# Three token tiles by gathered rows, and masks kept with the row of a group outermost, in a sparse feed-forward layer

## The chip, the cores and the metric

The kernel runs on one core of one Trainium2 chip. The metric is the device time of one launch in microseconds (us), the median of three runs. One more execution was taken with the hardware profiler; its rows are shown below, and all times inside the kernel come from it.

## What is computed

`x` is 16 x 100 x 1024, 1600 tokens. A cross-attention layer is added to it first; this text is about the sparse feed-forward layer behind it:

```python
def ffn(x, c1_w, c2_w, w1, w2t):              # 1600 tokens, DIM 1024, INTER 3584, SPARSITY 64, RANK 16
    inter = xf @ c1_w.T @ c2_w.T              # gate values, 1600 x 3584
    blk = inter.reshape(B * T, n_blocks, 64)  # 56 groups of 64 rows for each token
    idx = argmax(blk, axis=-1) + arange(0, INTER, 64)
    w1_g, w2_g = w1[idx], w2t[idx]            # one row of 64 is taken, for each token and group
    h = relu(einsum('bkm,bm->bk', w1_g, xf))
    return einsum('bk,bkm->bm', h, w2_g)
x = x + xattn(layernorm(x), ctx)
x = x + ffn(layernorm(x), c1_w, c2_w, w1, w2t)
```

## The kernel before

The layer is computed in two ways side by side. The tokens stand in tiles of 128; the first `S` tiles are the "sparse tiles", the rest go the dense way.

**The dense way.** `hidden_layer` multiplies the dense tokens with all 3584 rows of `w1` and closes what the gate did not choose; `project_down` multiplies the result with all of `w2t`. `w1` comes in 28 blocks of 128 rows, two of which are a pair (one pass of `body`, 14 in all). Each block is turned by TensorE (`turn_w`, L1669), and split into a high part by ScalarE (`high_part`, L1752) and a low part by VectorE (`low_part`, L1786). `sums` (L1698) is 24 matmuls (8 chunks x 3 products of high and low parts) over one of four column tiles of 336 tokens; `close` (L1689) adds a large negative number where the mask is set, as small bf16 matmuls with the mask as the stationary operand; ScalarE takes the tile out with Relu (`evacuate`, L1761), and it is stored in `h_scratch`.

**The masks.** For each pair TensorE makes the gate values of all 13 token tiles in four portions (`gates`, L1680; 4, 4, 4 and 1 tiles) in one two-bank tile of PSUM, so a portion waits until the one before has been read (the semaphore `compared`). On VectorE `pick` takes the maximum of each 64 (L1800), compares (L1802, writes bf16), multiplies by a falling key (L1804), takes the largest key (L1808), and `mark` compares again (L1817). All of the portion's four groups of a tile lie behind each other with the 64 rows innermost. `body` makes the masks of pair i + 1 while TensorE works on pair i, and `close` of the first tile of a pair waits for all its masks (`masked`).

**The gathered way.** For the S = 2 sparse tiles `SparseTiles` gathers, for each tile and each of 56 groups, the chosen row of `w1` for each token by an indirect DMA of GpSimd (L1529, 128 rows of 4 KB), and VectorE multiplies it with the token and sums (`dot`, L1536); later the chosen row of `w2t` is gathered and added with that weight (`axpy`, L1544). That is 112 dots and 112 sums. 78 dots (6 for each of 13 pairs) are done in `hidden_layer`, through a ring of 4 rows; 34 dots and all sums are spread over the units of `project_down`, through a ring of 6 rows. A row's buffer is gathered again when the step that read it is done.

**The second product.** `project_down` (L2376) goes in three passes over 28 chunks, with 11 token tiles in each (10 of 128 and one of 64), 66 units in all. ScalarE makes the high parts (L2292, L2283), VectorE the low parts (L2315, L2308), up to four units ahead of TensorE. The sparse steps stand between them in VectorE's order.

Each engine runs its instructions in the order in which they are written.

## Time and profile before

| what | us |
|---|---|
| median of three runs | 3539.28 (3535.36 to 3540.3) |
| profiled execution, its own time | 3539.46 |
| its span, first to last instruction | 3537.8 |
| hidden layer, about | 2605 to 3108 |
| second product, about | 3108 to 3538 |

A row of grouped instructions gives line, engine, operation, output and inputs with their shapes, how many, then busy time in us, the mean length of one in ns, and the idle time ahead of them with what ended it. Instructions of one engine overlap at their ends: the distance from start to start is what one costs when the engine is full, and is read from the timeline. "PE" is TensorE's matmuls, "PEld" its weight loads, "DVE" VectorE, "ACT" ScalarE, "POOL" GpSimd, "SPq" and "POOLq" transfers issued by SyncE and GpSimd.

### The profile page before, as it was taken

How to read it: one execution, taken by the hardware profiler on the slowest of the kernel's cores; microseconds unless marked ns; L12 is line 12 of the kernel's file. 1: busy time of each engine (PE TensorE's matmuls, PEld its weight loads, DVE VectorE, ACT ScalarE, POOL GpSimd, SP SyncE). 2: the span in 40 equal slices, each digit the busy share in tenths (PEclk: the TensorE clock that was granted, in tenths of full speed). 3: DMA queues.
4: the chain of work that ended last, by engine and by line, in shares of the span. 5: the costliest groups of instructions: out<-in, count | busy, mean ns of one | idle time of the engine just before them, and what ended most of it. 6: DMA issues, size and time to landing. Idle time of an engine off the chain costs nothing. (4 is left out here: it accounts for less than half of the span.)

```text
span 3537.8 us, 51963 instructions
## 1 busy us (share of the span) xinstructions
PE 3419.9 (97%) x18422; PEld 3044.1 (86%) x18422; DVE 2248.0 (64%) x3746; ACT 1372.0 (39%) x2610; POOL 877.6 (25%) x1108
## 2 busy tenths in 40 slices
PE   6999999799999999999999899999989999999999
PEld 5888888699999899999999778788789999977877
DVE  5555567677866577777777523433277787766775
ACT  4333344344433577777777422322231111121120
POOL 0000000000000477777776100000011111144543
PEclk8999999899999999999999999999999999999999
DMA  3333332354444334444333654544334444589786
GB/s 119 106 97 104 96 108 84 96 141 125 118 117 124 109 106 112 111 113 113 107 94 87 193 126 121 178 130 120 106 125 149 153 166 156 172 314 310 259 292 215
DMA packets 477970, 501.72 MB, mean 142 GB/s; under 512 B 172580, under 2 KB 372260, under 8 KB 477764
## 3 DMA queue, kind: packets, MB, share of 16 engines
q1 hardware_dynamic: 441988, 371.79, 36.0%
q0 software_dynamic: 34720, 125.19, 10.2%
q8 instruction: 117, 1.92, 0.2%
q10 hardware_dynamic: 1056, 2.10, 0.2%
q14 instruction: 89, 0.73, 0.1%
HBM read 383.98 MB, written 115.02 MB: 141 GB/s over the span
## 5 line engine op out<-in xcount | busy, mean ns | idle before, releaser
L2087 PE MATMUL wo_acc<-wo_w,wo_l 128*128 128x512 f32 (+1 forms) x2496 | 577.4, 393 | 17.0 <-DVE wo_l L2037 16.9
L269 PE MATMUL kv_bank<-kv_wo,kv_so 128*128 128x512 f32 x2436 | 575.0, 395 | 15.4 <-DVE kv_wo L361 11.1
L2087 PEld LDWEIGHTS wo_acc<-wo_w,wo_l 128*128 128x128 f32 (+1 forms) x2496 | 462.1, 186 | 132.2 <-DVE wo_w L2061 16.9
L269 PEld LDWEIGHTS kv_bank<-kv_wo,kv_so 128*128 128x128 f32 x2436 | 457.9, 190 | 110.4 <-issue 16.7
L657 PE MATMUL pr_bank<-pr_xo,pr_wp 128*128 128x400 f32 x2688 | 498.7, 347 | 29.0 <-ACT pr_s L724 13.4
L657 PEld LDWEIGHTS pr_bank<-pr_xo,pr_wp 128*128 128x128 f32 x2688 | 493.5, 190 | 31.8 <-DVE pr_wp L741 24.0
L1698 PE MATMUL hid_acc<-x1t,hid_w 128*128 128x336 f32 x2688 | 440.0, 319 | 0.0
L2376 PE MATMUL w_acc<-w_w,w_l 128*128 128x512 f32 (+1 forms) x1848 | 421.3, 390 | 5.2 <-DVE w_l L2315 5.2
L1698 PEld LDWEIGHTS hid_acc<-x1t,hid_w 128*128 128x128 f32 x2688 | 415.7, 189 | 1.1
L2376 PEld LDWEIGHTS w_acc<-w_w,w_l 128*128 128x128 f32 (+1 forms) x1848 | 339.0, 184 | 87.1 <-DVE w_l L2315 5.3
L2037 DVE TENSOR_TENSOR wo_l<-wo_l_raw,wo_l 128x512 fp32r<-128x512 f32 (+1 forms) x208 | 139.3, 671 | 344.5 <-ACT wo_l L2010 344.3
L27 PE MATMUL scores<-kt,q_parts 128*128 128x462 f32 x1152 | 338.7, 402 | 1.7 <-ACT probs L1218 1.7
L1089 POOL TENSOR_SCALAR probs<-probs,inverse 128x461 f32<-128x461 f32 x400 | 261.9, 655 | 210.0 <-DVE inverse L1256 172.4
L2010 ACT ACTIVATE wo_l<-wo_l_raw 128x512 fp32r<-128x512 f32 (+1 forms) x208 | 127.5, 614 | 408.5 <-PE wo_acc L2087 379.9
L1218 ACT ACTIVATE probs<-scores,negmax 128x461 f32<-128x461 f32 x400 | 258.0, 645 | 37.6 <-DVE negmax L1249 36.5
L1249 DVE TENSOR_REDUCE negmax<-scores 128x1 f32<-128x461 f32 x400 | 250.9, 627 | 23.8 <-PE scores L1126 23.2
L1142 PE MATMUL turned<-ident,probs 128*128 128x128 f32 x1600 | 241.1, 273 | 1.2 <-POOL probs L1089 1.2
L1142 PEld LDWEIGHTS turned<-ident,probs 128*128 128x128 f32 x1600 | 203.1, 142 | 20.2 <-POOL probs L1089 1.6
L1761 ACT ACTIVATE c_raw<-hid_acc 128x336 f32<-128x336 f32 x112 | 50.2, 452 | 392.1 <-PE hid_acc L1689 392.1
L27 PEld LDWEIGHTS scores<-kt,q_parts 128*128 128x128 f32 x1152 | 190.1, 192 | 10.7 <-ACT probs L1218 2.0
L1260 DVE TENSOR_TENSOR pt_first<-turned,pt_first 128x512 fp32r<-128x512 f32 x192 | 132.1, 688 | 86.2 <-ACT pt_first L1212 85.0
L1529 POOL DMA_INDIRECT w_ring<-in_L_ffn_w2t_dram,idx x112 | 141.8, 1266 | 162.8 <-DVE w_ys L1544 55.1
(194 smaller groups left out, 4581.0 us busy)
## 6 DMA issues: line engine op xcount, KB each, us to landing
wo_l_raw<-o_scratch SPq DMA_DIRECT2D x192, 256.0 KB, 2.9
pair_raw<-in_L_xattn_Wq_dram SPq DMA_DIRECT2D x64, 512.0 KB, 6.0
q_scratch<-pr_out SPq DMA_DIRECT2D x128, 200.0 KB, 2.6
o_scratch<-o_stage SPq DMA_DIRECT2D x64, 400.0 KB, 3.7
q_raw<-q_scratch SPq DMA_DIRECT2D x64, 384.0 KB, 3.1
stage<-in_ctx_dram SPq DMA_DIRECT2D x45, 512.0 KB, 4.0
h_scratch<-c_raw SPq DMA_DIRECT2D x28, 672.0 KB, 3.2
wo_w_raw<-in_L_xattn_Wo_dram SPq DMA_DIRECT2D x16, 1024.0 KB, 7.0
```

What stands on the lines that cost most here:

```text
L27: last = pe.matmul(out, left(a, c), right(b, c), start=(c == 0 and (a, b) == PAIRS[0]), stop=(c == chunks - 1 and (a, b) == PAIRS[-1]))
L269: last = pe.matmul(bank[:, BANK[i], :], so[:, i, a, c, :], wo[:, i, e, c, :], start=(not opened and c == 0 and (a, e) == PAIRS[0]), stop=( ...
L657: last = pe.matmul(bank[:, BANK[i], :width], wo[:, i, a, c, :], xo[:, i, e, c, :], start=(not opened and c == 0 and (a, e) == PAIRS[0]), s ...
L1089: pool.tensor_scalar(probs[:, I % RB, :kv], probs[:, I % RB, :kv], inverse[:, I % RB:I % RB + 1], 1.0, ALU.mult, ALU.mult).then_inc(scaled, 1)
L1142: last = pe.transpose(turned[:n, j % TB, k, :], probs[:, j % RB, at:at + n], ident[:, :])
L1218: act.activation(probs[:, I % RB, :kv], scores[:, I % SB, :kv], ACT.Exp, bias=negmax[:, I % RB:I % RB + 1], accum_out=total[:, I % RB:I % ...
L1249: dve.tensor_reduce(negmax[:, I % RB:I % RB + 1], scores[:, I % SB, :kv], AX.X, ALU.max, negate=True).then_inc(s_max, 1)
L1529: return pool.indirect_dma_start(row[:, :], None, (self.w1 if kind == "in" else self.w2t)[:, :], bass.IndirectOffsetOnAxis(self.idx[:, s, ...
L1698: pe.matmul(acc[:, t, :width], w[p][:, a, c, :], x1t[:, b, c, skip + t * width:skip + (t + 1) * width], start=(c == 0 and (a, b) == PAIRS[ ...
L2037: dve.tensor_tensor(l[j % 2][:, 1, :, :rows], l_raw[j % 2][:, :, :rows], l[j % 2][:, 0, :, :rows].bitcast(F32), ALU.subtract).then_inc(l_l ...
L2087: last = pe.matmul(acc[p][:rows, :], l[j % 2][:, a, k, :rows], w[:, c, m * per + k, :], start=(m == 0 and k == 0 and (a, c) == PAIRS[0]), ...
L2376: last = pe.matmul(acc[:heights[t], n % AB, h * cols:(h + 1) * cols], l[u % LB][:, a, k, :heights[t]], w[:, b, c % slots_w, h * cols:(h + ...
```

## The change

- S is 3: three token tiles go by gathered rows. The dense tokens are 1216 in place of 1344: a column tile has 304 columns in place of 336, and the second product has 10 token tiles in place of 11 (9 of 128 and one of 64), 60 units. Dots and sums are 168 each.
- All 168 dots are in `hidden_layer`, with one sum in each of 12 pairs: 180 steps for 13 pairs, 12 to 14 in one. The other 156 sums are in `project_down`. Both rings have 5 rows. The sums' accumulators (`totals`) are loaded at the start of `hidden_layer`.
- The masks are laid out with the row of a group outermost and the tiles' groups innermost, in two halves of 8 and 5 tiles. After the maximum (`largest`) ScalarE compares: one `Sign` activation for each tile and group (16 for a portion, 4 for the last) with the negated maximum as bias. VectorE then works on a half at a time: `keyed` adds the key, `halved` and `quartered` take maxima of the halves, `leading` reduces the 16 values left, `mark` compares. The leading key is bf16 now.
- ScalarE's `Sign` groups stand between its `evacuate` and `high_part`.
- The order of VectorE's work in a pair is written anew, with the steps between the parts of the masks.
- The normalised third tile is kept, and x1t holds the dense tokens alone.

```diff
-    R_HIDDEN, R_DOWN, PER_PAIR = 4, 6, 6
+    R_HIDDEN, R_DOWN, SUMS = 5, 5, 1
...
+            def signs(i, k):
+                a, n = picks[k]
+                x_half, at = divmod(2 * a, spans[0])
+                act.wait_ge(topped, NP * i + k + 1)
...
+                for x in range(n * per):
+                    last = act.activation(equal[x_half][:, x % pair, :, at + x // pair], values[:, x, :], ACT.Sign,
+                                          bias=top[:, a * per + x:a * per + x + 1])
+                last.then_inc(compared, 1)
...
+                    evacuate(i, p, 0)
...
+                    if another:
+                        high_part(j + 1, 1 - p, 0)
+                    if more and not late:
+                        signs(i + 1, 2 * p)
+                    evacuate(i, p, 1)
...
+                    if another:
+                        high_part(j + 1, 1 - p, 1)
+                    evacuate(i, p, 2)
+                    if more:
+                        signs(i + 1, 2 * p + 1)
+                    evacuate(i, p, 3)
...
-                dve.tensor_tensor(equal[:, at, :], values, spread(top[:, at], g), ALU.is_equal).then_inc(compared, 1)
...
+            def keyed(i, x):
+                dve.wait_ge(compared, NP * i + 2 * x + 3)
+                dve.tensor_tensor(equal[x][:, :, :, :], equal[x][:, :, :, :], key_bf[:, :, :spans[x]].rearrange(
+                    "q (b c) a -> q b c a", b=1).to_broadcast([P, pair, sparsity, spans[x]]), ALU.add).then_inc(step, 1)
+            def halved(i, x):
+                n, g = sparsity // 2, spans[x]
+                dve.wait_ge(step, 4 * (2 * i + x) + 1)
+                dve.tensor_tensor(half[:, :, :, :g], equal[x][:, :, :n, :], equal[x][:, :, n:, :], ALU.max).then_inc(step, 1)
...
+            def tree(i, m, x, between):
+                keyed(i, x)
+                steps(between[:1])
+                halved(i, x)
+                quartered(i, x)
+                steps(between[1:2])
+                leading(i, x)
+                steps(between[2:3])
+                mark(i, m, x)
+                if x == 0:
+                    indices(i)
...
+            def body(i, m, more):
+                mine = list(sparse.body[i])
+                cuts = (0, 2, 4, 9, 10, 10, len(mine)) if more else (0, 3, 6, 9, 12, 15, len(mine))
+                a, b, c, d, e, f = [mine[cuts[n]:cuts[n + 1]] for n in range(6)]
+                if i > 1:
+                    dve.wait_ge(clipped, i - 1)
+                low_part(2 * i + 1, 1, 0)
+                if more:
+                    largest(i + 1, 0)
+                steps(a)
+                low_part(2 * i + 1, 1, 1)
+                steps(b)
+                if more:
+                    largest(i + 1, 1)
+                steps(c)
+                if more:
+                    low_part(2 * i + 2, 0, 0)
+                    largest(i + 1, 2)
+                    tree(i + 1, 1 - m, 0, d)
+                    low_part(2 * i + 2, 0, 1)
+                    steps(e)
+                    largest(i + 1, 3)
+                    tree(i + 1, 1 - m, 1, f)
+                    steps(f[3:])
+                else:
+                    steps(d + e + f)
+                clip(i)
...
-        S = 2
+        S = 3
```

## Rows read from the trace of the kernel before

**Rows 1.** The page's first part: busy time, share of span, instructions of each engine.

```profile
PE 3419.9 (97%) x18422; PEld 3044.1 (86%) x18422; DVE 2248.0 (64%) x3746; ACT 1372.0 (39%) x2610; POOL 877.6 (25%) x1108
```

**Rows 2.** Windows: length, busy time of the engines, clock, DMA share, GB/s.

```profile
2605.00:3108.00 503.00, 494.95 (x3486) 477.30 (x3486) 388.08 (x523) 85.61 (x172) 78.83 (x81) 0.99 0.44 151
3130.00:3200.00 70.00, 70.00 (x310) 58.01 (x309) 55.50 (x64) 8.40 (x12) 50.28 (x37) 1.00 1.01 373
3200.00:3300.00 100.00, 100.00 (x442) 79.42 (x441) 72.07 (x83) 20.02 (x25) 43.19 (x35) 1.00 0.85 280
```

**Rows 3.** TensorE's timeline in the hidden layer: start, length, group, idle before.

```profile
2608.16 1.19 PE L1680 MATMUL gate<-c2s,zs 112*128 112x256 f32 x4 [1.77 <-DVE hid_w L1786]
...
2653.54 0.63 PE L1669 MATMUL turn<-ident,w_raw 128*128 128x128 f32 x4
...
2895.29 3.95 PE L1698 MATMUL hid_acc<-x1t,hid_w 128*128 128x336 f32 x24
2899.08 0.32 PE L1689 MATMUL hid_acc<-closed,hid_mask 128*128 128x128 bf16 x3
2899.24 0.63 PE L1669 MATMUL turn<-ident,w_raw 128*128 128x128 f32 x4
2899.62 0.72 PE L1680 MATMUL gate<-c2s,zs 112*128 x4
...
2930.39 0.88 PE L1698 MATMUL hid_acc<-x1t,hid_w 128*128 128x336 f32 x4
...
3108.82 9.54 PE L2376 MATMUL w_acc<-w_w,w_l 128*128 128x512 f32 x34 [5.18 <-DVE w_l L2315]
```

**Rows 4.** Groups of the second product, 3108 to 3538.

```profile
L2376 PE MATMUL w_acc<-w_w,w_l 128*128 128x512 f32 x1680 | 383.0, 390 | 5.2 <-DVE w_l L2315 5.2
L1544 DVE SCALAR_TENSOR_TENSOR w_ys<-w_ring,value,w_ys 128x1024 f32<-128x1024 f32 x112 | 140.1, 1280 | 12.4 <-DMA w_ring<-in_L_ffn_w2t_dram,idx 12.3
```

**Rows 5.** VectorE's timeline in one pair.

```profile
2894.55 1.22 DVE L1536 CUSTOM_DVE_ANT_0 c_raw<-c_raw,keep 128x1024 f32<-128x1024 f32 x1
...
2895.70 1.22 DVE L1536 CUSTOM_DVE_ANT_0 hid_ring<-hid_ring,keep 128x1024 f32<-128x1024 f32 x1
...
2900.53 0.69 DVE L1786 TENSOR_TENSOR hid_w<-turn,hid_w 128x512 fp32r<-128x512 f32 x1 [3.40 <-ACT hid_w L1752]
2901.14 1.21 DVE L1800 TENSOR_REDUCE hid_top<-gate 128x16 f32<-128x1024 f32 x1
```

**Rows 6.** VectorE's groups in the hidden layer, shapes apart.

```profile
L1808 DVE TENSOR_REDUCE hid_lead<-hid_equal 128x16 f32<-128x1024 bf16 x42 | 51.2, 1220 | 1.4
L1817 DVE TENSOR_TENSOR hid_mask<-hid_equal,hid_lead 128x1024 bf16<-128x1024 bf16 x42 | 51.2, 1218 | 0.6
L1800 DVE TENSOR_REDUCE hid_top<-gate 128x16 f32<-128x1024 f32 x42 | 51.1, 1218 | 8.8 <-PE gate L1680 8.8
L1804 DVE TENSOR_TENSOR hid_equal<-hid_equal,hid_key_bf 128x1024 bf16<-128x1024 bf16 x42 | 29.1, 692 | 1.4
L1808 DVE TENSOR_REDUCE hid_lead<-hid_equal 128x4 f32<-128x256 bf16 x14 | 5.9, 420 | 0.5
L1804 DVE TENSOR_TENSOR hid_equal<-hid_equal,hid_key_bf 128x256 bf16<-128x256 bf16 x14 | 4.1, 292 | 0.5
```

**Rows 7.** ScalarE's groups: two of the hidden layer, two of the attention.

```profile
L1761 ACT ACTIVATE c_raw<-hid_acc 128x336 f32<-128x336 f32 x112 | 50.2, 452 | 392.1 <-PE hid_acc L1689 392.1
L1752 ACT ACTIVATE hid_w<-turn 128x512 fp32r<-128x512 f32 x56 | 33.3, 598 | 25.0 <-PE turn L1669 24.0
...
L1218 ACT ACTIVATE probs<-scores,negmax 128x461 f32<-128x461 f32 x400 | 258.0, 645 | 37.6 <-DVE negmax L1249 36.5
...
L1190 ACT ACTIVATE kt<-kb 128x461 fp32r<-128x461 f32 x60 | 33.4, 557 | 0.0
```

**Rows 8.** ScalarE's timeline in the attention, two neighbours.

```profile
1501.72 0.59 ACT L1212 ACTIVATE pt_first<-turned 128x512 fp32r<-128x512 f32 x1
1502.20 0.65 ACT L1218 ACTIVATE probs<-scores,negmax 128x461 f32<-128x461 f32 x1
```

**Rows 9.** Transfers of the hidden layer: queues (packets, MB, share of 16 engines), issue to landing.

```profile
q0 software_dynamic: 11232, 40.90, 23.4%
q1 hardware_dynamic: 9465, 34.97, 20.7%
...
rows_raw<-in_L_ffn_w_dram,idx POOLq DMA_INDIRECT x38, 5.9
```

**Rows 10.** Transfers of the second product.

```profile
q0 software_dynamic: 21024, 76.56, 50.2%
q1 hardware_dynamic: 46439, 44.99, 32.2%
...
w_ring<-in_L_ffn_w_dram,idx POOLq DMA_INDIRECT x34, 7.0
```

**Rows 11.** TensorE's weight loads in the hidden layer.

```profile
L1698 PEld LDWEIGHTS hid_acc<-x1t,hid_w 128*128 128x128 f32 x2688 | 415.7, 189 | 1.1
...
L1689 PEld LDWEIGHTS hid_acc<-closed,hid_mask 128*128 128x128 bf16 x392 | 21.2, 98 | 16.1 <-DVE hid_mask L1817 0.5
```

**Rows 12.** The one table load of ScalarE after 2450.

```profile
L1433 ACT ACT_TABLE_LOAD x1 | 1.3, 1283 | 9.8 <-PEq L1902 9.8
```

More of the change, by code:

```diff
@@ L1315, in sb @@
             return mem.enter_context(nc.sbuf_tensor("mid_" + n, shape, dt))
[L1317 removed]
+        ring = list(lent) + [sb(f"raw{i}", [P, hidden]) for i in range(R - len(lent))]
         raw = [keep[t] if t < len(keep) else ring[t % R] for t in range(NT)]
@@ L1517, in __init__, with earlier @@
         sums = [("out", n % S, n // S) for n in range(S * groups)]
-        count = self.PER_PAIR * (groups // per - 1)
-        self.hidden, late = dots[:count], dots[count:]
-        self.down = []
-        for n, step in enumerate(sums):
-            self.down += late[len(late) * n // len(sums):len(late) * (n + 1) // len(sums)]
-            self.down.append(step)
-        self.pairs = groups // per - 1
-        where = {step: k for k, step in enumerate(self.down)}
-        assert all(("in", s, g) not in where or where["in", s, g] < where["out", s, g] for _, s, g in sums)
+        bodies = groups // per - 1
+        self.hidden, self.body = [], [range(0)]
+        for b in range(bodies):
+            first = len(self.hidden)
+            mine = dots[len(dots) * b // bodies:len(dots) * (b + 1) // bodies]
+            assert mine[-1][2] // per <= b + 1
+            self.hidden += mine
+            if b:
+                self.hidden += sums[self.SUMS * (b - 1):self.SUMS * b]
+            self.body.append(range(first, len(self.hidden)))
+        self.down = sums[self.SUMS * (bodies - 1):]
+    def earlier(self, steps, k):
+        return max([j for j in range(k) if steps[j][:2] == steps[k][:2]], default=None)
     def gather(self, pool, kind, s, g, row):
@@ L1565, in hidden_layer @@
     NP = len(picks)
+    assert NP == 4
+    pair = per // 2
+    spans = [sum(n for _, n in picks[2 * x:2 * x + 2]) * 2 for x in range(2)]
+    most = max(spans)
     parts = [[] for _ in range(tiles)]
@@ new lines, in steps, with first_pair @@
+            def steps(some):
+                for k in some:
+                    sparse_step(k)
+            def tree(i, m, x, between):
[9 more added lines that the diff above has]
+                    indices(i)
+            def first_pair():
+                for x in range(2):
+                    largest(0, 2 * x)
+                    largest(0, 2 * x + 1)
+                    tree(0, 0, x, ())
+                low_part(1, 1, 0)
+                low_part(1, 1, 1)
+                largest(1, 0)
+                largest(1, 1)
+                low_part(2, 0, 0)
+                largest(1, 2)
+                low_part(2, 0, 1)
+                tree(1, 1, 0, ())
+                largest(1, 3)
+                tree(1, 1, 1, ())
```

241 lines of the change are left out of this document (112 added, 129 removed).

## The prediction

> **What bounds the kernel now.** I read the page first: TensorE is busy for 97% of the span [rows 1]. The windows say the same of the two stages that the change touches: 495 of 503 us in the hidden layer, and 70 of 70 us in a stretch of the second product where the DMA engines are full [rows 2]. The timeline then gives the hidden layer's period. Pairs start at 2895.29 and 2930.39, 35.10 us apart, and nothing on TensorE waits between them [rows 3]. So before the change a column that TensorE does not compute is worth its time, as long as the other engines can follow. The question is whether they can, because the change gives them more.
>
> **What TensorE gets back.** In the second product 1848 matmuls of 512 columns are 168 for each of 11 token tiles; 383.0 us for 1680 is 0.228 us each [rows 4]. One tile fewer saves 168 x 0.228 = 38.3 us. In the hidden layer a tile of 24 matmuls of 336 columns takes 3.79 us to its close [rows 3], 0.158 us each. Between 336 and 512 columns a matmul grows by (228 - 158) / 176 = 0.40 ns a column; a column per cycle of the granted 2.4 GHz would be 0.42. For 32 columns I take 0.0133 us: 0.32 us for each of 112 tiles, 2.56 us a pair, 35.8 us in all. The closes are 26 for a pair, not 28, 0.1 us. TensorE's own pair would be 32.4 us.
>
> **What VectorE is given in a pair.** Costs from start to start. A dot is 1.15 us (2894.55 to 2895.70), a low part 0.61 (2900.53 to 2901.14) [rows 5]. From the lengths, less 0.08 of overlap: three maxima at 1.13 and one at 0.35, 3.75. The bf16 operations: the multiply takes 692 ns for 1024 elements and 292 for 256, which is 0.52 ns an element on 160 ns; the others (a reduce, or an f32 operand) take 1220 and 420, 1.04 ns an element on 160 [rows 6]. `keyed` and `mark` work on 2048 and 1280 bf16 elements: 1.15 and 0.75 each at the fast rate; 2.2 and 1.4 at the slow one. I take the fast one, because all operands are bf16 with the innermost step of one, as in the multiply. `halved` and `quartered` 0.73, 0.46 and 0.52, 0.25; `leading`, a reduce at the slow rate, 0.72 and 0.41. Indices 0.3, clip 0.2. The 13.85 steps (180 / 13) at 1.15 are 15.9. With 2.4 for low parts the sum is 29.5 us, before any wait. That is under 32.4, but VectorE's order is fixed, so the waits must be laid out.
>
> **What ScalarE is given.** A `Sign` of 64 columns reads PSUM with a bias for each partition. The activation of 461 columns with such a bias takes 645 ns, without it 557, and a column is 0.83 ns (598 against 452 for 512 and 336) [rows 7]: 0.65 - 397 x 0.00083 = 0.32 us. Two neighbours overlap by 0.11 (0.59 long, 0.48 apart) [rows 8], so 0.22 us apart. It could be 0.32 if the strided bf16 output stops the overlap, hardly less than 0.19. 52 in a pair are 11.4 us; with evacuations and high parts ScalarE has about 17 us. It is not the bound, but 16 in a row hold up what stands behind them for 3.5 us.
>
> **The pair, laid out.** Time 0 is the first low part of a body. `largest` 0 ends at 1.8; its 16 signs to 5.4, the evacuation 5.7, the high part 6.3: the second low part, which VectorE reaches at 4.0, starts at 6.4. A wait of 2.3. Two steps to 9.3, `largest` 1 to 10.4, then five steps. Here the ring of 5 counts: the fourth needs the buffer of a step that ended at 8.2. An indirect DMA takes 5.9 us to land at today's load and 7.0 in the second product [rows 9, 10]; the load will be near the latter, so I take 7.1 with the issue. The row is there at 15.3, a wait of 1.4. Five steps end at 17.6. Low part, `largest` 2, the first tree with its step, indices, low part: 25.6. `largest` 3 with its four signs holds `keyed` for 1.1 until 27.1. The second tree, with three steps, has its mask at 33.3. Now the close of the next pair's first tile runs, then `turn_w`, and the low part 1.29 us after that has begun (2899.24 to 2900.53) [rows 3, 5]: 0.05 + 0.16 + 1.29 on 33.3 is 34.8. TensorE reaches this close 3.47 us into its pair and waits some 2 us for it. So the pair is 34.8 us, set by maxima, signs, rows and masks, not by TensorE's 32.4. Of the 2.7 us saved, 0.3 is left. Bounds: 33.4 if rows never wait; 36.8 if signs are 0.32 apart (1.6 more) and rows land a little later.
>
> **Start and end of the hidden layer.** Before, 45.4 us lie between the first gate portion and the turn ahead of the first steady pair [rows 3]. Then no step is there to fill in. Each portion must wait for the one before to be reduced and compared, 1.2 + 3.5 us against 4.1 of TensorE's work, and the third portion's maximum is written behind the first tree, so TensorE idles some 5.5 us there; the masks come 6 us later than before. In the second pass three portions wait 1.5 us each and the first tree starts behind `high_part`, behind 16 signs; the close waits 3 us more. Less the shorter tiles this is 11 us lost (7 to 15). The last pair has no masks: 7 tiles after its first close save 2.2 us. Its 14 steps, at 5 rows in 8.3 us, end before TensorE does, so the next stage starts as before, 5.2 us after [rows 3].
>
> Hidden layer: +11 - 12 x 0.3 - 2.2 = +5 us.
>
> **The second product.** 156 sums in some 390 us. A gather holds the 16 DMA engines for 50.2% x 430 / 146 = 1.48 us; 156 of them are 231 us, and the rest, 32.2% x 430 less the eleventh tile, 128: 0.91 of the stage where it was 0.82 [rows 10]. In the first pass a step is due every 2.2 us, where 37 came in 70 us, 1.9 each, with TensorE full [rows 2]. VectorE's sum is 1.20, as long as 1.28 less the overlap [rows 4]. So this stage stays TensorE's, and I give 1 us to the first units, where rows come late. -37.
>
> Sum: 3539.5 + 5 - 37 = 3507.5, say 3508; the profiled execution and the median are the same within 0.2 us.
>
> **Two rules of the Trainium skill.** The masks are now read and written with a step of 32 or 20 bytes. No row shows that; a mask's load is 98 ns, an f32 block's 189 [rows 11], so at worst of these 26 closes cost 2.4 us more a pair, TensorE's 32.4 becomes 34.8, and the sum does not move but for 2 us of the last pair. The Trainium skill, "SBUF — State Buffer" (Door 1: The DMA port swizzle, its note on cachelines), says that each access that crosses to a new line pays a penalty, without a price; by it the closes, the signs and `leading` would all be slower than I count, and the sum larger by what that costs. Second, ScalarE's tables: after 2450 one load stands in the trace, 1283 ns ahead of the square root, and Copy and Relu alternate without any [rows 12]. The Trainium skill, "ScalarE: Activation LUTs" (Table sets: the hidden batching unit), says that a function of another set needs a load, and names Relu, Copy and Abs as in every set, but not Sign.
>
> **Rivals.**
> - A. As forecast: the small operations hold the pair at 34 to 36 us, the second product pays. 3498 to 3523. 57%.
> - B. The waits are shorter than I lay out (rows at 4 to 5 us, signs at 0.19), and TensorE bounds the pair at 32.4 to 33.2: 12 x 2.3 us less than 34.8, so 3480. For it: in the hidden layer the engines have room today [rows 2]. Against: the five steps in a row. 15%.
> - C. Slower than before: the bf16 operations on the new layout run at the slow rate. `keyed`, `halved`, `quartered`, `mark` cost 1.07 + 0.53 + 0.27 + 1.07 for the larger half and 0.67 + 0.33 + 0.16 + 0.67 for the smaller, 4.8 us, all in the chain: 39.6 us a pair, 12 x 4.8 + 4 at the start, 3569. It decides from a pair of 37.5 us on (37 - 11 + 2.2 = 28 us over 12 pairs). 10%.
> - D. Transfers: rows land 10 us after release; a pair is 37, and in the second product TensorE waits 8 us: 3508 + 26 + 8 = 3542. For it: 0.80 of the DMA engines in the hidden layer (13.85 x 1.51 + 7 in 34.8 us) against 0.44, with fewer rows in flight. 13%.
> - E. Sign stands in another table than Relu and Copy, and each change between them costs the 1283 ns of the row [rows 12]: two changes in each of the two sign groups on the path, 5.1 us a pair: 3508 + 61 = 3569. The trace shows nothing of Sign; for that Relu and Copy could be had beside it, one load would do and this falls away. 5%. It is the case that the rule of the Trainium skill's "ScalarE: Activation LUTs" leaves open.
>
> **Chances.** What this kernel's measurement can tell is about 0.2%, 7 us. Faster: A, B and a little of D, 0.80. Same 0.06, slower 0.14. The range takes in most of B and part of D: 3484 to 3536; the likeliest case alone is 3498 to 3523.
>
> **What would show it.** Right: pairs start 34 to 36 us apart, with one wait of about 2 us on the mask at the first close; VectorE over 90% busy in the hidden layer; `Sign` 0.22 apart; `mark` 1.2 us for 2048 elements; the second product 38 us shorter with TensorE full. Wrong: `mark` at 2.3 us (C), VectorE waiting for rows by several us a pair (D), table loads (E), pairs at 32.5 us (B), or a hidden layer whose start is not about 11 us longer.

## The result and the profile after

The changed kernel takes 3547.87 us (median of 11 runs, 3544.39 to 3551.22); the kernel before, measured beside it, 3539.52 (11 runs). The ratio is 1.0025, 95% interval 1.0015 to 1.0034: slower by some 8 us, just more than the 0.2% that can be told from no change. The forecast was 3508. The profiled execution took 3546.57 us with a span of 3544.9, 7.1 us more than before.

I read the stages first. The page's first part, beside [rows 1]:

```profile
PE 3365.6 (95%) x18226; PEld 2996.3 (85%) x18226; DVE 2272.8 (64%) x3815; ACT 1576.9 (44%) x3332; POOL 1065.9 (30%) x1220
```

TensorE has 54 us less to do and the span has not become shorter, so it waits. The windows, with the columns of [rows 2]: 505 us of the hidden layer, 59 us near its start, and the first 155 us of the second product.

```profile
2605.00:3110.00 505.00, 454.43 (x3254) 438.14 (x3255) 386.40 (x619) 286.08 (x887) 228.56 (x171) 0.96 0.68 236
2613.00:2672.00 59.00, 44.87 (x266) 43.24 (x266) 22.75 (x33) 34.72 (x116) 4.92 (x5) 0.82 0.19 66
3145.00:3300.00 155.00, 150.38 (x642) 120.45 (x643) 113.92 (x103) 29.80 (x37) 82.41 (x62) 0.96 0.96 335
```

In the hidden layer 50 us are idle on TensorE where 8 were [rows 2], and in the 59 us near its start the granted clock is 0.82. Laid against the trace of before, by the points that the forecast used (us; "turn" is the turn that follows a pair's first close):

| stretch | before | after | difference | forecast |
|---|---|---|---|---|
| first gate portion starts at | 2608.16 | 2610.98 | +2.8 | (in the next) |
| from there to the turn of the first steady pair | 45.38 | 65.12 | +19.7 | +11 |
| 12 pairs, turn to turn, mean of one | 35.10 | 36.40 | +15.7 | -3.6 |
| last pair, from its turn to its last close | 28.46 | 26.32 | -2.1 | -2.2 |
| from there to the second product | 5.63 | 6.28 | +0.7 | 0 |
| second product, first to last matmul | 420.88 | 390.01 | -30.9 | -37 |
| behind it | 8.06 | 9.30 | +1.2 | 0 |

The sum is +7.1, all of the difference between the spans. For the runs below, "start" and "pairs" are taken one tile of sums earlier, at the tile that stands ahead of a pair's first close: the start is 41.42 before and 59.20 here, and the pairs are 35.10 and 36.40 again.

Now one pair, on VectorE's timeline (start, length, line, operation, idle ahead). Its time 0 is 2931.11. Left out are mostly dots of 1.15 us each.

```profile
2931.11 0.69 DVE L1848 TENSOR_TENSOR hid_w<-turn,hid_w 128x512 fp32r<-128x512 f32 x1 [0.37 <-ACT hid_w L1779]
2931.71 1.21 DVE L1857 TENSOR_REDUCE hid_top<-gate 128x16 f32<-128x1024 f32 x1
...
2938.46 0.69 DVE L1848 TENSOR_TENSOR hid_w<-turn,hid_w 128x512 fp32r<-128x512 f32 x1 [3.25 <-ACT hid_w L1779]
...
2948.20 1.23 DVE L1546 CUSTOM_DVE_ANT_0 rows_raw<-rows_raw,keep 128x1024 f32<-128x1024 f32 x1 [1.05 <-DMA rows_raw<-in_L_ffn_w_dram,idx]
...
2949.36 0.69 DVE L1848 TENSOR_TENSOR hid_w<-turn,hid_w 128x512 fp32r<-128x512 f32 x1
...
2957.74 0.41 DVE L1857 TENSOR_REDUCE hid_top<-gate 128x4 f32<-128x256 f32 x1
2959.65 0.83 DVE L1862 TENSOR_TENSOR hid_equal<-hid_equal,hid_key_bf 128x1280 bf16<-128x1280 bf16 x1 [1.49 <-ACT hid_equal L1800]
...
2965.25 0.82 DVE L1883 TENSOR_TENSOR hid_mask<-hid_equal,hid_lead 128x1280 bf16<-128x1280 bf16 x1
...
2967.71 0.69 DVE L1848 TENSOR_TENSOR hid_w<-turn,hid_w 128x512 fp32r<-128x512 f32 x1 [0.36 <-ACT hid_w L1779]
```

It is the pair that was laid out, each wait at its place: low part 0, behind the signs at 7.35 (forecast 6.4); a row waited for, 1.05 (1.4); the third low part at 18.25 (17.6); the fourth maximum at 26.6 (25.6); `keyed` held 1.49 (1.1); the mask done at 34.96 (33.3); the next body at 36.60 (34.8). TensorE's timeline shows the wait at the end, ahead of the first close, and on ScalarE's stands what makes the first one:

```profile
2966.13 0.37 PE L1716 MATMUL hid_acc<-closed,hid_mask 128*128 128x128 bf16 x3 [2.25 <-DVE hid_mask L1883]
```

```profile
2932.96 4.74 ACT L1800 ACTIVATE hid_equal<-gate,hid_top 128x64 bf16<-128x64 f32 x16 [1.96 <-issue]
2937.20 0.76 ACT L1788 ACTIVATE c_raw<-hid_acc 128x304 f32<-128x304 f32 x1
```

Sixteen signs keep ScalarE for 4.24 us, 0.265 apart and not 0.22. The evacuation behind them takes 0.63 us up to the high part, where the forecast had 0.3.

TensorE's own work in such a pair, its length less its idle time, is 33.1 to 33.3 us. In five of the 12 pairs a part of it runs at 1.2 GHz behind the wait at the first close, and it is 34.4 to 34.6 us.

The groups, shapes apart (2610 to 3142), give the prices of the masks:

```profile
L1800 ACT ACTIVATE hid_equal<-gate,hid_top 128x64 bf16<-128x64 f32 x728 | 223.1, 761 | 124.7 <-DVE hid_top L1857 115.6 <-issue 9.1
...
L1883 DVE TENSOR_TENSOR hid_mask<-hid_equal,hid_lead 128x2048 bf16<-128x2048 bf16 x14 | 17.2, 1225 | 0.5
L1862 DVE TENSOR_TENSOR hid_equal<-hid_equal,hid_key_bf 128x2048 bf16<-128x2048 bf16 x14 | 17.0, 1217 | 4.7 <-ACT hid_equal L1800 4.7
L1877 DVE TENSOR_REDUCE hid_lead<-hid_quarter 128x32 bf16<-128x512 bf16 x14 | 16.7, 1189 | 0.5
```

`mark` and `keyed` run at the fast rate as forecast. `leading`, 512 elements, takes 1.19 where 0.69 would follow from the length. The start of the layer, on TensorE (the second to fourth tile of sums and what stands ahead of each):

```profile
2618.26 0.71 PE L1707 MATMUL gate<-c2s,zs 112*128 112x256 f32 x4 [1.89 <-ACT hid_equal L1800]
2618.81 3.50 PE L1725 MATMUL hid_acc<-x1t,hid_w 128*128 128x304 f32 x24
2625.00 1.19 PE L1707 MATMUL gate<-c2s,zs 112*128 112x256 f32 x4 [2.69 <-ACT hid_equal L1800]
2625.99 5.79 PE L1725 MATMUL hid_acc<-x1t,hid_w 128*128 128x304 f32 x24
2635.99 0.55 PE L1707 MATMUL gate<-c2s,zs 112*128 112x256 f32 x1 [4.22 <-ACT hid_equal L1800]
2636.35 5.73 PE L1725 MATMUL hid_acc<-x1t,hid_w 128*128 128x304 f32 x24
```

After idles of 2.69 and 4.22 us 24 matmuls take 5.8 us in place of 3.5: the granted clock has gone from 2.4 to 1.2 GHz. Up to the first steady pair six idles on ScalarE's signs add to 14.1 us (1.89, 2.69, 4.22, 2.19, 0.69, 2.39), and five slow tiles (4.39, 5.79, 5.73, 5.12, 5.03, each less 3.5) to 8.6. The first of these tiles stands behind an idle of 3.76 us ahead of the first portion. The second product, on TensorE:

```profile
3145.56 138.51 PE L2469 MATMUL w_acc<-w_w,w_l 128*128 128x512 f32 x600 [5.78 <-DVE w_l L2418]
3288.13 12.20 PE L2469 MATMUL w_acc<-w_w,w_l 128*128 128x512 f32 x42 [4.06 <-DVE w_w L2411]
```

The first pass is 10 of the 28 chunks, 600 matmuls for 10 token tiles. So the one wait, 4.06 us, stands between the first pass and the second, ahead of the new weights (`w_w`). Behind it 42 matmuls take 12.2 us where 42 x 0.228 is 9.6; the granted clock there is 1.2 GHz again. What led to the wait, on ScalarE and VectorE:

```profile
3281.66 0.74 ACT L2395 ACTIVATE w_l<-rows_raw 128x640 fp32r<-128x640 f32 x1 [4.24 <-DMA rows_raw<-h_scratch]
3282.31 1.04 ACT L2386 ACTIVATE w_w<-w_raw 128x1024 fp32r<-128x1024 f32 x1
...
3283.18 1.28 DVE L1554 SCALAR_TENSOR_TENSOR total<-w_ring,value,total 128x1024 f32<-128x1024 f32 x1
...
3284.37 2.47 DVE L1554 SCALAR_TENSOR_TENSOR total<-keep,value,total 128x1024 f32<-128x1024 f32 x2
...
3286.76 1.22 DVE L2411 TENSOR_TENSOR w_w<-w_raw,w_w 128x1024 fp32r<-128x1024 f32 x1
```

The weights themselves were there. Late was a tile of `h`, 12.3 us from its issue (3269.38) to its use, which holds ScalarE. Then the high part of the weights is ready at 3283.35, and VectorE starts their low part at 3286.76, because three sums stand ahead of it in its order.

### The profile page after: what moved, and what is told of

Its sections match the earlier page's. It is cut to its first block and busy times, and to the rows that moved or that the text cites. A ratio compares the mean times of both kernels' runs of the same rounds, so it can differ in the third digit from the quotient of the medians.

```text
span 3544.9 us, 52710 instructions
## 1 busy us (share of the span) xinstructions
PE 3365.6 (95%) x18226; PEld 2996.3 (85%) x18226; DVE 2272.8 (64%) x3815; ACT 1576.9 (44%) x3332; POOL 1065.9 (30%) x1220
## 5 line engine op out<-in xcount | busy, mean ns | idle before, releaser
L1725 PE MATMUL hid_acc<-x1t,hid_w 128*128 128x304 f32 x2688 | 411.7, 310 | 0.1
L2469 PE MATMUL w_acc<-w_w,w_l 128*128 128x512 f32 (+1 forms) x1680 | 386.3, 393 | 9.8 <-DVE w_l L2418 5.8
L1725 PEld LDWEIGHTS hid_acc<-x1t,hid_w 128*128 128x128 f32 x2688 | 391.2, 195 | 1.3 <-DVE hid_w L1848 0.3
L2469 PEld LDWEIGHTS w_acc<-w_w,w_l 128*128 128x128 f32 (+1 forms) x1680 | 309.4, 184 | 86.4 <-DVE w_l L2418 5.9
L1800 ACT ACTIVATE hid_equal<-gate,hid_top 128x64 bf16<-128x64 f32 x728 | 223.1, 761 | 124.7 <-DVE hid_top L1857 115.6
L1218 ACT ACTIVATE probs<-scores,negmax 128x461 f32<-128x461 f32 x400 | 258.2, 646 | 38.0 <-DVE negmax L1249 36.8
L2100 POOL DMA_DIRECT2D x_scratch<-wo_y x26 | 14.5, 557 | 577.3 <-DVE wo_y L2154 555.5
```

What stands on the lines that cost most here:

```text
L1218: act.activation(probs[:, I % RB, :kv], scores[:, I % SB, :kv], ACT.Exp, bias=negmax[:, I % RB:I % RB + 1], accum_out=total[:, I % RB:I % ...
L1725: pe.matmul(acc[:, t, :width], w[p][:, a, c, :], x1t[:, b, c, t * width:(t + 1) * width], start=(c == 0 and (a, b) == PAIRS[0]), stop=False)
L1800: last = act.activation(equal[x_half][:, x % pair, :, at + x // pair], values[:, x, :], ACT.Sign, bias=top[:, a * per + x:a * per + x + 1])
L2469: last = pe.matmul(acc[:heights[t], n % AB, h * cols:(h + 1) * cols], l[u % LB][:, a, k, :heights[t]], w[:, b, c % slots_w, h * cols:(h + ...
```

## The experiments

All are the changed kernel with one edit, unless it says otherwise; times are medians, ratios are against the kernel before.

My theory: the forecast's mechanisms are the right ones and its prices too low. The chain of signs, maxima, rows and masks in VectorE's order holds each pair (36.4 against TensorE's 33.3), and the start adds idle time that costs the clock as well. Rivals: TensorE's work itself has become longer by the stepped mask loads; the transfers hold the pair; the prices of the small operations alone do it, in any order.

**e1: small operations by themselves.** A kernel that computes nothing of the reference: groups of 16 activations of 64 columns, 16 reduces, and 64 loads and matmuls.

> A kernel of its own that measures single operations and computes nothing of the layer (its output is zeros). ScalarE, 16 at a time, 64 columns from PSUM: Sign with a bias for each partition to bf16 with a step of 16; the same to bf16 in a row; Relu without such a bias in a row, and with a step; Copy in a row; Sign from SBUF. VectorE: 16 reduces of 512 bf16 elements to 32 with the 16 that are reduced a step of 16 apart, then with them in a row. TensorE: 64 bf16 matmuls of 128 columns whose stationary operand is in a row, has a step of 16, or of 10. In the changed kernel 16 Sign are 4.24 us from the first to what follows, 0.265 apart, and the reduce of 512 took 1.20 us. If the stepped write is what costs, the first group is 0.26 apart and the second 0.22; if the function or the bias costs, both are 0.26 and Relu 0.19 or less. The reduce: 1.2 with the step, 0.69 in a row if the step costs; 1.2 both if bf16 output or shape does. Mask loads: in the changed kernel a close of three takes 0.05 us longer; expected 0.06 apart in a row and 0.075 with a step.

ScalarE's timeline: L112 is Sign with a bias into places 32 bytes apart, L116 the same in a row, L120 Relu without bias in a row, L124 that with the step.

```profile
6.85 4.53 ACT L112 ACTIVATE wide<-values,bias 128x64 bf16<-128x64 f32 x16
11.41 3.38 ACT L116 ACTIVATE flat<-values,bias 128x64 bf16<-128x64 f32 x16
14.82 1.97 ACT L120 ACTIVATE flat<-values 128x64 bf16<-128x64 f32 x16
16.82 4.44 ACT L124 ACTIVATE wide<-values 128x64 bf16<-128x64 f32 x16
```

```profile
L100 DVE TENSOR_REDUCE lead<-wide 128x32 bf16<-128x512 bf16 x16 | 15.7, 1056 | 22.4 <-ACT wide L132 22.4
...
L103 DVE TENSOR_REDUCE lead<-flat 128x32 bf16<-128x512 bf16 x16 | 9.6, 675 | 0.0
```

A sign is 0.255 us apart from the next with the stepped output, 0.20 in a row; Relu 0.25 and 0.10. With the step the bias makes no difference, so it is the stepped write that sets the pace. A reduce of 512 values costs 0.97 us stepped and 0.59 in a row. The mask loads with their matmuls were 62 ns apart with the step of 16 and 59 with that of 10 (medians). Of the block in a row the first 38 were 107 ns apart, and the rest 56: between them the granted clock rose from 1.2 to 2.4 GHz.

**e2: another order in the pair.** Each half's masks are finished before steps stand behind them, and the two halves' signs have five steps for cover.

```diff
-                steps(a)
+                steps(mine[:5])
                 low_part(2 * i + 1, 1, 1)
-                steps(b)
...
-                steps(c)
+                steps(mine[5:10])
...
-                    tree(i + 1, 1 - m, 0, d)
+                    tree(i + 1, 1 - m, 0, ())
                     low_part(2 * i + 2, 0, 1)
-                    steps(e)
                     largest(i + 1, 3)
-                    tree(i + 1, 1 - m, 1, f)
-                    steps(f[3:])
+                    steps(mine[10:11])
+                    tree(i + 1, 1 - m, 1, ())
+                    steps(mine[11:])
```

> The changed kernel with VectorE's order in a pair alone altered: five steps ahead of the second low part, five behind the second maximum, none inside the trees, one between the last maximum and its keyed, the rest behind the last mask. Same work, same rows, same rings. Theory 1 (the pair's length is the chain maximum, signs, trees with steps between, mask, close, turn, low part): the mask is there before TensorE asks for it, the pair falls from 36.4 to 33 us, TensorE waits under 0.5 us a pair, 3507. Rival 2 (rows and transfers set the pace): the same 14 rows come through the same ring, pairs stay over 35.5 us, 3537 to 3548. Rival 3 (TensorE is slower by the stepped mask loads and idles for other reasons): pairs 36, no change.

3522.57 us, ratio 0.9963 (0.995 to 0.9977). Pairs are 34.35 us, 2.05 less, with every operation and every transfer as before the edit; start (59.3) and second product (392.9) hardly moved. The theory had 33 us and 3507, so little more than half of its gain came. The list of waits of 2680 to 3100 says what changed. In the changed kernel (engine, what for, us, times, longest):

```profile
DVE hid_w L1848 <- ACT hid_w L1779: 44.7, 24, 3.3
...
PE hid_acc L1716 <- DVE hid_mask L1883: 22.8, 11, 2.2
```

In e2 the wait on the mask is gone and the second has shrunk; rows are waited for instead, 9.1 + 5.6 + 4.8 us:

```profile
DVE hid_w L1848 <- ACT hid_w L1779: 9.2, 12, 0.8
DVE rows_raw L1546 <- DMA rows_raw<-in_L_ffn_w_dram,idx: 9.1, 14, 2.5
```

So it is not the prices alone, nor TensorE's work: the order around them made them wait for each other. In these 12 pairs TensorE is never at the low clock, where five of the changed kernel's are in part.

**e3: another order at the start.** Three maxima go ahead of the first tree, the third portion's signs of pair 1 stand behind the high part, and VectorE takes up the wait for GpSimd's keys behind its first low parts.

```diff
-                for x in range(2):
-                    largest(0, 2 * x)
-                    largest(0, 2 * x + 1)
-                    tree(0, 0, x, ())
+                for k in range(3):
+                    largest(0, k)
+                dve.wait_ge(made, 2)
+                dve.wait_ge(base_made, 1)
+                tree(0, 0, 0, ())
+                largest(0, 3)
+                tree(0, 0, 1, ())
```

> The changed kernel with the start of the hidden layer alone altered: the third maximum of the first pair ahead of the first tree, the wait for the keys that GpSimd makes ahead of the first tree and not ahead of the first low part, and ScalarE's high part ahead of the third group of signs in the second block. Theory: gate values to the first steady turn falls from 65.1 to about 55 us (4.6 for the tree, 3 for the keys, the rest clock): 3536. Rival (16 signs in a row and the half clock bound the start whatever the order): 3545 or more.

3538.06 us, ratio 1.0002 (0.9993 to 1.0011). The start is 55.5, 3.7 less, and pairs stay at 36.2. From the first portion to the first steady turn are 59.1 us, where the theory had 55. The first portion starts at 2607.2, 3.7 us sooner, but only 1.3 of this is the edit's: from the layer's first turn to the first portion are 3.52 us here, 4.83 in the changed kernel and 2.83 before. The rest is an earlier start of the whole layer in this execution.

**e4: the masks alone.** S is 2 as before; masks, signs and order are as in the changed kernel, and all dots (112 now) are in the hidden layer.

```diff
-        S = 3
+        S = 2
```

> The changed kernel with S = 2 (two sparse tiles, 112 dots and 112 sums, all dots in the first product; one more row buffer of its own, as the borrowed one is too short): the masks, ScalarE's compares and the order without the third tile. Theory 1: nothing waits on masks in a steady pair, pairs 35.1 + 0.6 for the stepped mask loads = 35.7; the start is 22 us longer than before; the second product is 421 us as before: 3540 + 22 + 7 = 3569. Then the third tile is worth 21 us and the masks cost 29. Rival (the third tile itself costs more than it gives): 3547 or less.

3573.35 us, ratio 1.0101 (1.0086 to 1.0117): 36 us slower than before. The third tile by itself then gives some 27 (an estimate, from the two ratios). The second product is 421.3, as before; the start is 58.6, as in the changed kernel, so that all of its loss belongs to the masks. The pairs are 35.85, all alike but for the first, and on TensorE nothing waits in them:

```profile
2944.69 0.39 PE L1716 MATMUL hid_acc<-closed,hid_mask 128*128 128x128 bf16 x3
2944.91 0.64 PE L1696 MATMUL turn<-ident,w_raw 128*128 128x128 f32 x4
...
2963.60 3.85 PE L1725 MATMUL hid_acc<-x1t,hid_w 128*128 128x336 f32 x24
```

Three closes now take 0.22 us up to the next operation, where they took 0.16 [rows 3], and the whole pair 35.85 where it was 35.10 with the same tiles: the stepped masks cost TensorE 0.75 us a pair. The rival of the longer TensorE work has that much of it; in the changed kernel it makes 32.4 into some 33.1, still under the chain. e5 below bears it out with masks in a row: there three closes take 0.15 us, and TensorE's own work in a pair at full clock is 32.2 us.

**e5: the row of a group innermost.** The signs write in a row, `leading` reads in a row, and the masks lie as before the change; the maxima by halves and the order stay.

```diff
-        equal = [sb(f"equal{x}", [P, pair, sparsity, g], BF16) for x, g in enumerate(spans)]
+        equal = [sb(f"equal{x}", [P, g * pair, sparsity], BF16) for x, g in enumerate(spans)]
...
-                    last = act.activation(equal[x_half][:, x % pair, :, at + x // pair], values[:, x, :], ACT.Sign,
+                    last = act.activation(equal[x_half][:, 2 * at + x, :], values[:, x, :], ACT.Sign,
```

> The changed kernel with the masks laid out as before it, the 64 rows innermost, and all else kept (maximum by halves, ScalarE's Sign, bf16 key and lead). Signs are then written in a row: 16 in 3.4 us, not 4.3 (the single operations were 0.20 and 0.25 apart); the reduce 0.4 and 0.25 us shorter; mark spreads its lead over the innermost axis and goes at the slow rate, 1.07 and 0.67 us longer. Theory (these single prices add up along the chain): a steady pair 36.4 - 0.85 - 0.15 - 0.65 + 1.75 = 36.5, the start 5 us shorter for its signs and 2.6 for the keys: 3540. If only mark matters the pair is 38 and it is 3567; if only the signs matter 35.5 and 3530.

3537.84 us, ratio 1.0004 (0.9995 to 1.0013). The start is 50.2, 9 us shorter; the pairs are 36.37, as long as in the changed kernel, and the second product is 391.5. The groups show a bargain with a loss: sixteen signs take 3.38 us, `leading` 0.69, but `mark` has doubled.

```profile
L1799 ACT ACTIVATE hid_equal<-gate,hid_top 128x64 bf16<-128x64 f32 x728 | 154.9, 358 | 120.9 <-DVE hid_top L1856 113.9 <-issue 7.1
...
L1882 DVE TENSOR_TENSOR hid_mask<-hid_equal,hid_lead 128x2048 bf16<-128x2048 bf16 x14 | 32.1, 2291 | 0.5
...
L1876 DVE TENSOR_REDUCE hid_lead<-hid_quarter 128x32 bf16<-128x512 bf16 x14 | 9.6, 686 | 0.5
```

Here `mark`'s second operand repeats one value along the innermost axis, 2.29 us for 2048; in the changed kernel it is repeated along a middle one, 1.22. The Trainium skill, "VectorE: DVE Perf Modes" (Mode 2×_1P), wants 16-bit operands with a step of one for the double rate; both rows agree.

**e6: 52 sums left out.** Of the second product's sums those of the third tile are not done, which leaves a part of the output out.

```diff
-        self.down = sums[self.SUMS * (bodies - 1):]
+        self.down = [x for x in sums[self.SUMS * (bodies - 1):] if x[1] != 2]
```

> The changed kernel without the third tile's sums in the second product (it leaves 52 of the 156 out, so the third tile's output lacks them). At the rate of before, 0.228 us a matmul, the second product's 1680 matmuls are 383 us; they take 390 to 392. Theory: the 7 to 9 us are lost to transfers (DMA engines 0.94 to 0.97 busy in its first pass, rows and weights late): with a third fewer gathers it is 383 to 385, the whole 3540. Rival (TensorE restarts at half its clock, or VectorE is late for other reasons): 389 or more.

3540.62 us, ratio 1.0008 (0.9999 to 1.0017). The second product takes 383.5 us, 1680 x 0.228 almost to the tenth, and nothing waits in it: what is lost there hangs on the sums and their gathers. The edit takes both away and can't tell them apart. At the start of the second pass VectorE takes up the new weights 0.04 us after ScalarE has made their high part, with no sum in between.

**e7: the order of e2 with a ring of 6 rows.**

```diff
-    R_HIDDEN, R_DOWN, SUMS = 5, 5, 1
+    R_HIDDEN, R_DOWN, SUMS = 6, 5, 1
```

> The new order of VectorE's work (e2) with a ring of 6 rows in the hidden layer. With 5 rows pairs were 34.35 us and VectorE waited 19 us for rows between 2680 and 3100, 1.6 us a pair, TensorE 32.7 of work. Theory (the ring is what is left): pairs 33.2, 3509. Rival (the DMA engines are full, a sixth row lands no earlier; or the signs hold the gate values): 34.2 and 3521.

3540.49 us, ratio 1.0005 (0.9995 to 1.0016), 15 us slower by the ratios than e2 with one row less; theory and rival both missed. Pairs run from 32.7 to 38.9 us. In the list of waits stands a new one, of ScalarE ahead of an evacuation:

```profile
ACT c_raw L1789 <- remote: 32.5, 7, 4.9
```

It is not explained. In the case that I take as an example, the evacuation starts at 2838.12. The close that it follows had ended at 2833.78, and the store of `h` of two blocks earlier, issued at 2813.35, had its last packet 5.3 us later, at 2818.7. Nor do the stores take longer with a sixth row. From the records of their packets, issue to last packet, they take 2.9 to 3.7 us in the kernel before (median 3.1), 2.7 to 7.2 in the changed kernel (6.5), 4.1 to 6.9 in e2 (5.6) and 2.9 to 7.0 here (5.4). So what makes e7 slower than e2 stays open.

**e8: a ring of 7 rows in the second product.**

```diff
-    R_HIDDEN, R_DOWN, SUMS = 5, 5, 1
+    R_HIDDEN, R_DOWN, SUMS = 5, 7, 1
```

> The changed kernel with a ring of 7 rows in the second product, not 5. If what is lost there (390 to 392 us against 383) is the wait of VectorE for single rows, 7 rows give back some 5 us: 3543. If the DMA engines' time is what is short, more rows in flight take it from the weights and the left tiles: 390 or more, 3548.

3547.72 us, ratio 1.003 (1.0018 to 1.0042), the second product 389.8: nothing gained, so a deeper ring does not help. The wait, 3.23 us here, stands at the same place, ahead of the second pass, with three sums of VectorE ahead of the low part of the new weights: their high part is ready at 3283.97, and the low part starts at 3287.38.

**e9: e2 and e3 together.**

> This joins the order of run e2 (each half's masks finished early, rows and signs behind them) with the start of run e3, on the changed kernel. My theory, that the waits inside a pair and the idle TensorE at the start are separate losses, adds them up: pairs of about 34.4 us as in e2 and a start of about 56 us as in e3, so 3522.6 - 4 to - 9: about 3515 (3512 to 3520). Rival: the start's loss is the low clock and not the order of the first portions, so nothing more is gained than e3's steady pairs hid: 3519 to 3523.

3514.06 us, ratio 0.9932 (0.9918 to 0.9946). Pairs 34.13, start 52.7: the two losses add. The second product is longer, 395.9, with waits of 4.7 and 3.8 us, one ahead of each of the later passes.

**e10: e9 with the layout of e5.**

> The same with the row of a group innermost, as the masks were laid out before the change, all operations as in the changed kernel. In run e5 that layout made the start 9 us shorter (50.2 against 59.2) and left the pairs as long as they were. If it acts on the start by its cheaper operations (compares in a row, a reduce without a step), it adds to the order: start 47 to 51 us, pairs 34.3, about 3508 (3503 to 3514). Rival: with the order of the start already put right there is nothing for it to save, 3513 to 3517, or its halves' maxima bring the slower pairs (36.4) back: 3535.

3500.94 us, ratio 0.9893 (0.9877 to 0.9909), below both ranges. Start 46.3, pairs 33.67, second product 389.8. Of the 13 us against e9 the start gives 6.4 and the pairs 5.5. The second product gives another 6.1, though the layout touches nothing in it, and the layer starts 5 us later in this execution. With `mark` at 2.29 us the layout is still the better one once the order no longer puts VectorE on the path at the first close. In the second product the high part of the second pass's weights is ready at 3234.56, 5.7 us before the first pass ends, and VectorE starts the low part only at 3241.83, behind four more sums, a low part of `h` and a wait of 1.1 us for a row; TensorE waits 2.88 us. TensorE's timeline at the start: the same three portions as above,

```profile
2619.03 0.64 PE L1706 MATMUL gate<-c2s,zs 112*128 112x256 f32 x4
2619.50 3.50 PE L1724 MATMUL hid_acc<-x1t,hid_w 128*128 128x304 f32 x24
2624.50 0.71 PE L1706 MATMUL gate<-c2s,zs 112*128 112x256 f32 x4 [1.50 <-ACT hid_equal L1799]
2625.05 3.52 PE L1724 MATMUL hid_acc<-x1t,hid_w 128*128 128x304 f32 x24
2630.04 0.36 PE L1706 MATMUL gate<-c2s,zs 112*128 112x256 f32 x1 [1.48 <-ACT hid_equal L1799]
2630.24 3.48 PE L1724 MATMUL hid_acc<-x1t,hid_w 128*128 128x304 f32 x24
```

with no idle over 1.5 us between the tiles, and none of these tiles at the low clock.

**e11: e10 with fewer sums in the first pass.**

```diff
-    room = [0 if u % PER in (2, 3) or u < 2 else groups[q][g][1] - groups[q][g][0]
+    room = [0 if u % PER in (2, 3) or u < 2 else (groups[q][g][1] - groups[q][g][0]) * (3 if q == 0 else 4)
```

> As the run before, with the 156 sums of the second product spread with fewer of them in its first pass (weight 3 against 4 in the two others), where the w_w loads come on top. If the 7 us that the second product is longer than 1680 x 0.228 are transfers that collide in the first pass, 2 to 4 us less than the run before. Rival: the total of the transfers counts, not their place: the same within 1 us.

3501.9 us, ratio 0.9899 (0.9883 to 0.9915), no gain. The second product by itself is 393.7, 3.9 longer than in e10. TensorE now goes from the first pass to the second without a wait, and the wait stands ahead of the third. Again sums of VectorE stand between the high part of the weights, ready at 3355.41, and their low part, started at 3362.57:

```profile
3137.76 221.77 PE L2466 MATMUL w_acc<-w_w,w_l 128*128 128x512 f32 x976
3363.94 71.54 PE L2466 MATMUL w_acc<-w_w,w_l 128*128 128x512 f32 x300 [4.40 <-DVE w_w L2408]
```

**e12: two activations for sixteen.** The comparison is left out, each group's first row is always taken.

```diff
-                for x in range(n * per):
-                    last = act.activation(equal[x_half][:, x % pair, :, at + x // pair], values[:, x, :], ACT.Sign,
-                                          bias=top[:, a * per + x:a * per + x + 1])
+                for b in range(pair):
+                    last = act.activation(equal[x_half][:, b, :, at:at + 2 * n].rearrange("q c a -> q a c"),
+                                          values.rearrange("q (a b) c -> q b a c", b=pair)[:, b, :2 * n, :],
+                                          ACT.Relu, scale=0.0)
```

> The changed kernel, with the 16 (or 4) Sign activations of a portion replaced by 2 activations of the whole portion with scale 0, so that each group's first row is always taken: this leaves the comparison out, and the output is not the reference's. Everything else (order, masks, rows, transfers) stays. It shows what the small activations on the path cost. My theory: in each pair two of the sign groups are waited for, and 4.2 us of each become about 1.3; the first wait is wholly in the pair, the others partly, so pairs of 33.5 us (32.5 to 34.5) where they are 36.4, the start 4 to 8 us shorter, in all about 3505 (3495 to 3515). Rival: rows and the order of the chain bound the pair and the time gained before the first low part is lost at the rows: pairs of 35.5 to 36.4, about 3530 to 3545.

3556.65 us, ratio 1.0051 (1.0034 to 1.0067). Pairs are 37.1, the second product 397.1. It did not take the cost away, so it could not show what the pair would be without it, and both theories of the expectation rest on a premise that the trace refutes. With the first row always taken, all tokens also gather the same row of a group, so more than the signs differs here; why it is slower than the changed kernel stays open. ScalarE's timeline in a pair:

```profile
2938.84 4.67 ACT L1800 ACTIVATE hid_equal<-gate 128x512 bf16<-128x512 f32 x2 [1.96 <-DVE hid_top L1858]
```

Two instructions for 1024 columns keep ScalarE as long (4.67 us) as sixteen did (4.74). The price is by the stepped column: (4.67 - 2.53) / 512 = 4.2 ns, and 0.265 / 64 = 4.1 ns with the signs; in a row a column is 0.83 ns [rows 7]. With a stepped output, then, cutting the work into small instructions costs next to nothing.

## Why the prediction was wrong

The forecast had the change 32 us faster; it is 8 us slower. No rival came true: the bf16 operations of the masks did not go to the slow rate (C), no table was loaded in the hidden layer (E), rows were waited for 1 us a pair and not by several (D), TensorE was not the bound (B). Of D the loss of 8 us in the second product came near (7). Case A was right in what happens and wrong in how much: the step that failed is the sizes of three terms, the pair, the start and the second product, which came out some 39 us too low together. One of its signs was off from the outset: VectorE was to be over 90% busy in the hidden layer, where the forecast's own 29.5 us of 34.8 are 85%; it was 315 of 380 us (2700 to 3080), 83%.

- **The pair, 34.8 forecast, 36.4 measured: 12 x 1.6 = 19 us.** The largest error, made of small ones on one chain. In the pair shown, 1.8 longer than laid out: +0.95 at the second low part, 0.7 of it from signs 0.265 apart where I took 0.22 and the rest from the evacuation behind them (0.63 for 0.3); -0.3 from a shorter wait for the row; +0.4 and +0.2 in the two trees, from `leading` (1.20 and 0.73 for 0.72 and 0.41); +0.4 at `keyed`, signs again; +0.14 around the close. The bounds of this term, 33.4 to 36.8, did hold the result; the range of the total did not take in their upper end together with the errors of the other terms. I had taken the pace of the signs from activations that write in a row and left the step to the upper bound; for TensorE's loads I had allowed 2.4 a pair at worst (e4 shows 0.75), and for `leading` nothing. The Trainium skill's rule on lines that I had weighed there ("SBUF — State Buffer", Door 1: The DMA port swizzle) is on any access that crosses to a new line, so it holds for signs and `leading` too. e1 agrees with it, and puts the price at 0.055 us a sign and 0.38 us for 512 values.
- **The start, 11 forecast, 22.5 measured (2.8 + 19.7).** The idle time was counted about right: 14.1 us on signs and 2.1 at the first steady close, where the forecast's pieces come to some 13. What was missing is the clock. Five of the tiles run in part or wholly at 1.2 GHz, 8.6 us in all, where before one did (5.96 for 3.85, 2.1 us); the forecast had no term for it. Of the 2.8, 2.0 are GpSimd's key table, which has 1024 entries now (64 before; 2.79 us where it took 0.24) and holds VectorE's first low part; I had not listed it among what the change moves. The other 0.8 is a later start of the layer. e3 takes 1.3 off the wait for the keys and 3.7 off the start.
- **The last pair, -2.2 forecast, -2.1 measured.** This term was right.
- **The second product, -37 forecast, -30.9 measured, and +1.2 behind it.** 1680 matmuls would take 383.0. I had found room for 156 gathers by shares (0.91 of the engines) and gave 1 us; 7 are lost, 4.06 in the one wait ahead of the second pass and 2.6 in the low clock behind it. e6 gets them back with 52 sums fewer, e8 does not with more rows in flight, and e11 moves the wait from the second pass to the third. Two things lead to it in the changed kernel: a tile of `h` that lands late, with the DMA engines 0.96 busy up to 3300, and VectorE's order, which puts three sums ahead of the low part of the new weights. The order there is that of the kernel before, where VectorE's sums were done in time (high part ready at 3254.72, low part started at 3254.75). In e10 the tile of `h` no longer holds the high part, and TensorE still waits 2.88 us. The forecast weighed transfers here and not this order. An edit that puts these sums behind the low parts was not run, so how much of the 7 us each one makes is not shown. The 1.2 are behind the last matmul, where a third tile of totals is to be stored.

The strongest evidence that the order, and not the amount of work, costs most is e2: the same instructions in another order are some 22 us faster (0.9963 against 1.0025). With the start and the layout as well (e10) the change is worth 38 us, about half of the 74 us of TensorE's work that the forecast counted (38.3 + 35.8).

## What to carry to other kernels

When work moves off the engine that bounds a kernel, the gain is only there if the chain through the other engines is shorter than that engine's own work. Lay this chain out with prices for the exact access patterns, then move what is waited for (maxima, signs, masks) ahead of what can wait (dots, sums). A layout change has a price on each engine that writes or reads it: check the innermost step of every operand, and measure it in a small kernel before it is built in. Long waits on TensorE have tiles at the low clock behind them: at the start of this layer four waits of 2.2 to 4.2 us cost 7.7 us more in the tiles behind them, and two of 0.7 and 1.9 us none. Where a stage changes its weights, look at what stands ahead of them in each engine's order.

## What the runs showed of the hardware

- ScalarE writes bf16 at 4.1 to 4.2 ns a column when neighbours are 32 bytes apart, as 16 instructions or as 2, and with or without a bias; 64 columns in a row cost 0.10 us without a bias and 0.20 with Sign and a bias (e1, e12).
- A reduce of 512 bf16 values on VectorE takes 0.97 us from start to start with that step, 0.59 in a row (e1).
- A bf16 comparison with an operand repeated along the innermost axis takes 2.29 us for 2048 elements, along a middle axis 1.22 (e5 and the changed kernel).
- bf16 weight loads of 128 x 128 with their matmuls of 128 columns are 56 ns apart in a row, 62 with a step of 32 bytes and 59 with one of 20, at 2.4 GHz (e1). In the hidden layer three closes take 0.15 us in a row (e5) and 0.22 stepped (e4).
- Sign, Relu and Copy alternate without a table load between them: one load of 1283 ns ahead of all six groups of e1, and none in the hidden layer of the changed kernel.
- The plain stores of `h` reach their last packet later in the kernels with more gathers: median 3.1 us after issue in the kernel before (6 dots a pair), 6.5 in the changed kernel (12 to 14 steps a pair). A sixth row in the ring did not add to it (5.4 in e7, 5.6 in e2).
